# A two-layer gated cross-attention kernel: the first head's operand rows copied by matrix products, the mask's sum moved to GpSimd behind the head loads

## What is computed

```python
qh = (q @ Wq.T + bq); kh = (k @ Wk.T + bk); vh = (v @ Wv.T + bv)   # k = v = ctx, 6404 x 128
attn = softmax(einsum('bhtd,bhsd->bhts', qh, kh) * scale)           # 1024 x 6404 per head
out = einsum('bhts,bhsd->bhtd', attn, vh) @ Wo.T + bo
x = x + tanh(g_xattn) * out                                         # then the experts, gated too
```

## Time and profile before

| | us |
|---|---|
| median of three timed runs (2675.59 to 2676.3) | 2675.84 |
| the profiled execution, its own time | 2680.53 |
| its span, first to last instruction | 2678.5 |
| PE busy | 2498.9 |
| DVE busy | 2157.2 |
| ACT busy | 1935.9 |
| GpSimd busy | 27.6 |

### The profile page before, as it was taken

The page is one execution under the profiler, slowest core; times in us unless marked ns, Lnnn a source line. Parts: engine busy times, 40 slices in busy tenths (PEclk is TensorE's granted clock), DMA queues, the critical chain, the costliest instruction groups (busy, mean ns, idle before and its releaser), DMA issues.

```text
span 2678.5 us, 50842 instructions
## 1 busy us (share of the span) xinstructions
PE 2498.9 (93%) x21050; PEld 959.8 (36%) x21052; DVE 2157.2 (81%) x2215; ACT 1935.9 (72%) x3545; POOL 27.6 (1%) x27
## 2 busy tenths in 40 slices
PE   3379999999999999999796899999999999999989
PEld 1243333333333333334342333333333333333343
DVE  5469999999999999953436899999999999999144
ACT  2058888888888888885331388888888888888932
POOL 4000000000000000000000000000000000000000
PEclk9559999999999999999796799999999999999989
DMA  7120000000000000003100000000000000000000
GB/s 250 69 82 21 29 29 29 29 29 29 28 28 28 29 29 29 22 25 117 54 1 22 4 30 28 28 28 28 28 28 30 29 29 29 28 28 14 1 0 8
DMA packets 36417, 94.36 MB, mean 35 GB/s; under 512 B 4020, under 2 KB 14808, under 8 KB 35928
## 3 DMA queue, kind: packets, MB, share of 16 engines
q1 hardware_dynamic: 34744, 90.69, 9.3%
q10 hardware_dynamic: 1440, 0.40, 0.1%
HBM read 75.08 MB, written 15.74 MB: 34 GB/s over the span
## 4 chain that ended last, share of the span: by engine, by line
PE 63%; DVE 32%; SPq 2%; DMA 1%; issue 1%; ACT 1%; DVEq 0%; ACTq 0%
DVE m_part L657 29%; PE ps L978 22%; PE ps L930 19%; PE ps L949 9%; PE ps L1079 4%; PE ps L1087 3%; SPq L299 1%; PE ps L890 1%; PE ps L920 1%; DMA probs<-in_mask_t 1%; PE ps L882 1%; DVE probs L613 1%; SPq L308 1%; PE ps L992 1%; PE ps L1099 1%
## 5 line engine op out<-in xcount | busy, mean ns | idle before, releaser
L657 DVE TENSOR_REDUCE m_part<-ps 128x2 f32<-128x1024 f32 (+1 forms) x1664 | 1933.1, 1184 | 168.2 <-PE ps L949 164.0
L495 ACT ACTIVATE probs<-ps 128x512 f32<-128x512 f32 (+1 forms) x3264 | 1760.0, 595 | 313.8 <-PE ps L930 197.8
L978 PE MATMUL ps<-probs,v_all 128*9 128x256 f32 x13056 | 1010.8, 382 | 1.6 <-ACT o_raw L475 0.5
L930 PE MATMUL ps<-q_ring,k_ring 35*128 35x512 f32 x3264 | 872.1, 497 | 0.6 <-ACT q_ring L484 0.4
L949 PE MATMUL ps<-k_ring,q_ring 33*128 33x512 f32 (+1 forms) x3328 | 732.2, 419 | 63.2 <-DVE m_part L657 34.6
L930 PEld LDWEIGHTS ps<-q_ring,k_ring 35*128 35x128 f32 x3264 | 348.5, 183 | 709.1 <-ACT probs L495 612.3
L949 PEld LDWEIGHTS ps<-k_ring,q_ring 33*128 33x128 f32 x3328 | 350.0, 194 | 150.7 <-DVE m_part L657 107.1
L978 PEld LDWEIGHTS ps<-probs,v_all 128*9 128x9 f32 x13056 | 195.3, 89 | 549.2 <-ACT probs L495 465.3
L794 DVE TENSOR_TENSOR probs<-probs,ps 128x512 f32<-128x512 f32 x64 | 39.7, 682 | 77.6 <-ACT probs L528 70.1
L528 ACT ACTIVATE probs<-ps,b_col 128x512 f32<-128x512 f32 x64 | 44.0, 687 | 72.3 <-PE ps L1079 72.2
L678 DVE RECIPROCAL r_den<-ps 128x8 f32<-128x8 f32 x32 | 6.6, 207 | 107.0 <-PE ps L957 106.7
(11 more groups left out here) (127 smaller groups left out, 590.3 us busy)
## 6 DMA issues: line engine op xcount, KB each, us to landing
k_ring<-k_parts SPq DMA_DIRECT2D x384, 96.0 KB
k_ring<-k_parts SPq DMA_DIRECT2D x128, 112.2 KB
probs<-in_mask_t SPq DMA_DIRECT2D x10, 640.0 KB, 4.5
k_parts<-probs SPq DMA_DIRECT2D x12, 512.0 KB, 3.1
k_parts<-big SPq DMA_DIRECT2D x12, 512.0 KB, 3.1
q_ring<-q_parts SPq DMA_DIRECT2D x120, 32.0 KB
big<-in_w SPq DMA_DIRECT2D x1, 2048.0 KB, 10.5
q_parts<-probs SPq DMA_DIRECT2D x4, 512.0 KB, 3.5
```

What stands on the lines that cost most here:

```text
L495: A(probs[0:k, n % PSLOTS, HALF * half:HALF * half + HALF], ps[0:k, e_bank(unit), :], ACT.Exp, scale=SCALE).then_inc(sem(f"exp_done{l}"), 1)
L657: V.tensor_reduce(m_part[:, h % 2, :, p, c], mx(n % 2)[:, :, 0:chunk_w[c]], AX.X, ALU.max).then_inc(sem(f"mx_done{l}"), 1)
L930: pe.matmul(bank, k_ring[row:row + ROWS_EXP, koff:koff + P], q_ring[row:row + ROWS_EXP, qoff:qoff + HALF], start=not masked, stop=True).th ...
L978: mm = pe.matmul(ps[32 * g:32 * g + VW, 7, 0:QGW], v_all[:, t, h, :], probs[:, n % PSLOTS, QGW * g:QGW * g + QGW], start=(t == 0), stop=(t ...
```

## The change

1. Head 0's rows of layer 0 no longer pass through HBM. PE multiplies the staged parts by 0/1 matrices (`r_k`, `r_q`, made by GpSimd in `selections`) that put each channel on all its rows (`repeat`), into bank 6, and ACT copies the bank to the ring (`copy_over`), adding the ones row as a bias. The key chunks are made inside the loop of the first units, three chunks ahead. The staging buffers lie in the part of `k_ring` that belongs to head 1.
2. The low part of layer 0's keys is made by GpSimd (`low_keys`) from a second ACT copy with the bias (`k_sum`) instead of by DVE from PSUM.
3. Each attention weight has its own wait (`weight_in`) in place of one for all eight loads; the bias rows of the two layers share one buffer, layer 1's being loaded behind its first head's loads.
4. SP issues the other small loads and the first experts' weights (`setup`) after head 0 and 1's loads, not before.
5. GpSimd clears and sets ring rows only once the normalised x is there, and its other constants come behind the third chunk's low part, with a single semaphore.
6. The mask's pieces are loaded one behind each head's key loads (heads 2 to 12); GpSimd adds them as 32-bit integers and folds the sum to 160 words, DVE totals those.
7. `m_pad` becomes fp32r and the four transposes of the row step become plain fp32r products with an fp32r identity. The PE warming products read `zeros` in place of `probs`.

The diff, cut to its core:

```diff
             def load_first0():
 
-                sp.wait_ge(sem("ring_set"), RING_SET)
-                first_queries(0)
-                store_k(0)
-                keys_stored(0)
-                for g in range(len(K_GROUPS)):
-                    load_keys(0, 0, g)
-                sp.wait_ge(sem("q_stored0"), 16 * 2)
-                load_queries(0, 1)
-                for g in range(len(K_GROUPS)):
+                store_q(0)
+                for g, (c0, c1) in enumerate(K_GROUPS):
+                    store_k(0, c0, c1)
+                    if g == 0:
+                        sp.wait_ge(sem("ring_set"), RING_SET)
+                        sp.wait_ge(sem("q_stored0"), 16 * 2)
+                        load_queries(0, 1)
+                        sp.wait_ge(sem("copied_over"), REPEAT_AT["q"] + 1)
+                        keys_stored(0, c1)
+                        load_keys(0, 1, g)
+                keys_stored(0)
+                sp.wait_ge(sem("copied_over"), NCH + 1)
+                for g in range(1, len(K_GROUPS)):
                     load_keys(0, 1, g)
                 load_queries(0, 2)
...
                         load_keys(l, h, g)
+                    if l == 0 and h - KRING <= NFULL // MCH:
+                        check_mask(h - KRING)
...
+            load_context()
+            load_first0()
             setup()
-            load_first0()
-            check_mask()
             load_heads(0)
...
             constants()
+            for c in range(NCH):
+                low_keys(c)
+                if c == 2:
+                    more_constants()
+                if c == UPPER:
+                    pool.wait_ge(sem("copied_over"), REPEAT_AT["q"] + 1)
+                    pool.wait_ge(sem("q_stored0"), 16 * 2)
+                    set_ones(0, HALF * UPPER, 0)
+            pool.wait_ge(sem("copied_over"), NCH + 1)
+            for n in range(KST):
+                pool.wait_ge(sem(f"k_stored0_{n}"), 16 * len(range(n, NCH, KST)))
+            set_ones(HALF * UPPER, TK, 2)
+            put_mask_together()
...
+            def project_k(c):
+
+                w = chunk_w[c]
+                act.wait_ge(sem("k_proj0"), c + 1)
+                if c >= KST:
+                    act.wait_ge(sem(f"k_stored0_{c % KST}"), 16 * (c // KST))
+                    act.wait_ge(sem("repeated"), REPEAT_AT[c - KST] + 1)
+                A(k_st[0][:, c % KST, 0, 0:w], ps[:, 4 + c % 2, 0:w], ACT.Identity, bias=b_col[:, 0, 1:2]).then_inc(sem("k_evac0"), 1)
+                if c >= 2:
+                    act.wait_ge(sem("k_split0"), c - 1)
+                A(k_sum[:, c % 2, 0:w], ps[:, 4 + c % 2, 0:w], ACT.Identity, bias=b_col[:, 0, 1:2]).then_inc(sem("k_evac0"), 1)
+
+            def copy_over(what):
+
+                act.wait_ge(sem("repeated"), REPEAT_AT[what] + 1)
...
+                    A(k_ring[:, HALF * what:HALF * what + chunk_w[what]], ps[:, 6, 0:chunk_w[what]], ACT.Identity,
+                      bias=one_rows[:, 0:1]).then_inc(sem("copied_over"), 1)
...
-            project_q(0)
-            project_k()
-            for c in range(NCH):
-                set_v(c)
-                if c < NFULL // MCH + 1:
-                    sum_mask(c)
-            act.wait_ge(sem("mask_summed"), NFULL // MCH + 1)
             exp_all(0)
...
             def maxima(l):
-                dve.wait_ge(sem("rank"), E + 4)
+                dve.wait_ge(sem("constants"), 1)
...
+            def repeat(what):
+
+                n = REPEAT_AT[what]
+                pe.wait_ge(sem("selected"), 4 * PARTS)
+                if n:
+                    pe.wait_ge(sem("copied_over"), n)
+                if what == "q":
+                    pe.wait_ge(sem("q_split0"), 2)
+                    for i in range(2 * PARTS):
+                        mm = pe.matmul(ps[:, 6, :], r_q[:, i, :], q_st[0][0:HD, i // PARTS, i % PARTS, :],
+                                       start=(i == 0), stop=(i == 2 * PARTS - 1))
+                else:
+                    pe.wait_ge(sem("k_split0"), what + 1)
...
                     for p in range(NPAIR):
-                        mm = pe.transpose(bank[:, P * p:P * p + P], m_pad[:, p, :], ident_f[:, :])
+                        mm = pe.matmul(bank[:, P * p:P * p + P], m_pad[:, p, :], ident_r[:, :], start=True, stop=True)
...
             def attention(l, masked):
                 for i, unit in enumerate(FIRST_UNITS):
+                    if l == 0 and i % 4 == 0 and i // 4 + 3 < NCH:
+                        keys(0, i // 4 + 3, 4)
+                    if l == 0 and i % 4 == 1 and i // 4 + 2 < NCH:
+                        repeat(i // 4 + 2)
                     m_unit(l, unit, masked)
...
-                    if l == 0 and i % 4 == 3 and i // 4 < NCH:
-                        values(0, i // 4, 4, 4)
+                    if l == 0 and i % 4 == 2 and i // 4 < NCH:
+                        values(0, i // 4, 7, 1)
...
+            turn_queries(0)
+            keys(0, 0, 4)
             queries(0)
-            for c in range(NCH):
-                keys(0, c)
+            keys(0, 1, 4)
+            repeat(0)
+            repeat("q")
+            keys(0, 2, 4)
+            repeat(1)
             attention(0, False)
```

More of the change, by code:

```diff
@@ L78 @@
 K_GROUPS = [(0, 3), (3, 6), (6, 9), (9, KCH)]
+UPPER = 6
+REPEATS = [0, "q"] + list(range(1, KCH))
+REPEAT_AT = {u: n for n, u in enumerate(REPEATS)}
+RING_SET = KRING + 2
+MASK_LEFT = 160
 def max_units(h):
@@ L322, in first_queries @@
                             row = HB * half + (b * PARTS + part) * HD
-                            sp.dma_start(q_ring[row:row + HD, 0:HALF].bitcast(F32), q_st[0:HD, half, part, :].bitcast(F32)
+                            sp.dma_start(q_ring[row:row + HD, 0:HALF].bitcast(F32), q_st[l][0:HD, half, part, :].bitcast(F32)
                                          ).then_inc(query_in(l, 0)[0], 16)
@@ new lines, in put_mask_together @@
+            def put_mask_together():
+                words = mask_sum.bitcast(I32)
+                link(nc.gpsimd.memset(mask_sum, 0.0))
+                for c in range(NFULL // MCH + 1):
+                    pool.wait_ge(sem(f"mask_in{c % 2}"), 16 * (c // 2 + 1))
+                    rows, n = (P, MCH * TQ // 4) if c < NFULL // MCH else (TAIL, TQ // 4)
+                    new = sum_stage[c % 2].bitcast(I32)[0:rows, 0:n]
+                    if c:
+                        pool.wait_ge(sem("mask_met"), c)
+                    nc.gpsimd.tensor_tensor(words[0:rows, 0:n], words[0:rows, 0:n], new, ALU.add).then_inc(sem("mask_met"), 1)
+                pool.wait_ge(sem("mask_met"), NFULL // MCH + 1)
+                n = MCH * TQ // 8
+                while n > MASK_LEFT:
+                    link(nc.gpsimd.tensor_tensor(words[:, 0:n], words[:, 0:n], words[:, n:2 * n], ALU.add))
+                    n //= 2
+                nc.gpsimd.tensor_tensor(words[:, 0:n], words[:, 0:n], words[:, n:2 * n], ALU.add).then_inc(sem("mask_folded"), 1)
@@ L872, in _, with keys @@
         def _(pe):
-            def keys(l, c):
+            def keys(l, c, bank):
                 w = chunk_w[c]
+                if c == 0:
+                    pe.wait_ge(*weight_in(l, "k"))
                 if l == 0:
```

258 lines of the change are left out of this document (163 added, 95 removed).

## The result

The changed kernel takes 2612.97 us (median of four runs, 2605.52 to 2616.61) against 2675.72 for the kernel before beside it: a ratio of 0.9764, 95% interval 0.9742 to 0.9787. (The ratios compare all the repeated runs of both kernels, so they can differ by some tenths of a per cent from the quotient of the medians.) Its profiled execution took 2612.98 with a span of 2611.2, which is 67.3 less than the span of before.

The account below looks back on a forecast made before the run. PE paces most of the span, so the gain must come from the first 190 us: 46 (start) + 33.6 (mask) + (72.9 - 64.7) (units) = 88, less 2 for rows, 86; 2680.5 becomes 2594.5, less 4.7, 2590; range 2576 to 2618.

Parts of the forecast that it names:

- rival (a): Head 0's units: PE's slow clock stays throughout, maxima end at 112, 18 us worse, total 2608; chance 0.17.
- The start: Up to the first reduction: normalised x at 10.3, first reduction at 29 (27 to 33) against 75.11, 46 us earlier.
- The mask: Head 0's units: the 33.6 us halt goes whole; GpSimd's additions, at most 3.3 us each, cost nothing.
- rival (c): GpSimd's mask additions meet DVE's SBUF operations in ten heads: 33 us, total 2623; chance 0.05.
- The row products: Row step, 32 times in the full loop: fp32r products replacing transposes cost between 0 and 16 us; 2 taken.
- rival (b): Row step: the products cost the plain f32 price, 14 us more than taken, total 2604; chance 0.09.
- The pace of the units: Head 0's 52 units: clock rises after one 6.8 us group, then nine at 4.8; 64.7 us in all.
- the 88: End of head 0's maxima: at 94 against 181.62, 88 us earlier, from start, mask halt and units.
- the 4.7 us: Whole kernel: the runs' median stands 4.7 us below the profiled execution, so 2594.5 becomes 2590.
- The low end of the range: Whole kernel: start at 27, all groups at 4.7, no row cost; 98 us gained, 2578, rounded to 2576.
- (d): Head 0's units: the copies' ring through PE, ACT and GpSimd paces the groups, 70 us more, 2660; chance 0.03.
- (e): Loop: warming with zeros fails to lift PE's clock; two heads at 1.2 GHz give 2722, slower than before; chance 0.02.

Follow-up runs that it names:

- before_no_mask_sum: The kernel before without mask loads and sums, the total that picks layer 1's path set by hand: 2642.26 us, ratio 0.9813.
- after_no_mask: The changed kernel without the mask's loads and GpSimd's additions, layer 1's path picked by a constant: 2608.64 us, ratio 0.9722.
- after_again: The changed kernel unaltered, executed once more as a reference: 2612.14 us, ratio 0.9783.
- fill3: The changed kernel with one 512-column bf16 product of zeros ahead of each key chunk, copying product and value chunk, three per group of four units: 2594.83 us, ratio 0.9679.
- constants_first: The changed kernel with GpSimd's other constants made behind the first key chunk's low part instead of the third's: 2606.14 us, ratio 0.9736.
- all_warm: The changed kernel with zero products in unit groups, early constants, warmed last heads, and one warming product behind late layer 0 units and layer 1's first-head units: 2608.43 us.

## Why the prediction was right, and where it was wrong

The forecast was 2590 in a range of 2576 to 2618; 2613 is inside it, 23 above. The direction held, and so did the mechanism of the start and of the mask. The mechanism of the units' pace did not: 2613 is inside because the range was drawn to reach rival (a), whose 2608 is nearer than the forecast.

- **The start: right.** Normalised x 10.49 (10.3 foretold), first reduction 29.77 (29), with the constants last. GpSimd's subtraction took 1.27 us, not 1.0, the constants 26.62 to 29.74, 3.1 and not 3.5. The estimate of 1.1 from the Trainium skill (GPSIMD Engine Reference, section 3.1) was nearer than mine, and still low. A weight did come late: PE's L1049 waited until 13.51 for Wq. I had costed the separate waits at nothing, and it stayed in the range.
- **The mask: right.** Of the halt of 33.59, 32.3 come back where nothing else changes (before_no_mask_sum), and the additions are hidden (after_no_mask): rival (c) didn't happen.
- **The row products: better than taken.** 0 in place of 2: the bound of the 260-wide row was the true one, and rival (b) fell. Its 16 us also came from a misread row: the 1.41 us counts from a weight load at 1237.08 that stands ahead of the products. PE's timeline of the kernel before there:

```profile
1237.51 1.05 PE L890 MATMUL ps<-w_att,ctx_t 128*128 128x128 f32 x8
```

The next product began at 1238.49, so the eight take 0.98 us, 0.39 more than the four transposes and not 0.82.
- **The pace of the units: wrong.** The step that failed is "I expect it to rise after the first group and stay for the nine with key chunks". The clock came up for about 3 us in three of the groups and fell back (in after_again for three groups in a row, in none of these traces for all nine). The price of a group at the full clock was right: 4.8 foretold, 4.83 and 4.87 in after_again. What is more, the pieces at the slow clock were undersized: chunk 2.0 for 1.7, copies 1.14 for 1.0, pairs 0.72 or 0.57 for 0.5, which makes 7.75 and not the 6.8 of rival (a). The last two groups took 5.98, as foretold. From first reduction to end the units took 115.71 - 29.77 = 85.9 us and not 64.7: 21.2 more. With the start's 0.8 that is the 88 that became 65.9.
- The reason given for the step was that the group would be full. It was: PE 77.21 of 80 us busy. The flaw was to let that decide. The row that spoke against it, a clock of 0.50 with PE at 76%, came from the stage next in kind, as the prediction said of rival (a); the full loop is quite another mix of products. Rival (a) had 0.17; it is what happened for the most part, its end of 112 (115.71 measured, 110.45 in after_again) included.
- **The other terms.** From 86 to 67.3 there are 22.1 for the above, 2 back for the row products, 2.15 for head 1, 5.1 back between the layers, 1.6 at the end: 22.1 - 2 + 2.15 - 5.1 + 1.6 = 18.8. Nobody foretold the 5.1, and whether the change has earned it is not shown: that stage took 324.9 to 337.6 us in the traces of the changed kernel and its variants, and 329.2 to 337.2 in those of the kernel before. It is luck that it helped. And the 4.7 us that I took off because before's profiled execution lay above its median did not recur: the changed kernel's two agree. 18.8 + 4.7 is the 23. The low end of the range does not add up either: start at 27, groups at 4.7 and no row cost give 48.1 + 33.6 + 13.8 = 95.5, not 98.
- Rivals (d) and (e) didn't show. The ring of copies was fast enough with DVE pacing at 5.08 us (fill3), and the loop from 140 us on has a clock of 1.00 with zeros as the warming data.

**Open.** Why the clock rises in some groups and not in others, and why three fillers hold it up (a wait of 0.24 us for DVE does not by itself bring it down, as after_again shows); the size of what constants_first gives by itself; what lets it fall in the last head in some executions only.

## What to carry to other kernels

When two pieces of a profile differ in clock, price the new stage at both, and let only a row of the same mix decide: "PE is full" is not such a row. Where PE paces a stage at the lower clock, a few products of zeros between its pieces can be worth more than they cost (three per group of four units gave 14 to 17 us here), but try them stage by stage: in layer 1 a unit became 0.14 us longer by them. And taking away an interference that is plain in the trace (22 us of memsets beside the norm) may pay nothing while what caused it only moves to another place on the path.

## What the runs showed of the hardware

- The granted clock can sit near 0.5 with PE busy for 19.77 of 20 us, and even for 30.00 of 30 (all_warm, layer 1), and stand at 1.00 with 20.00 of 20 (fill3): the busy share of the trace does not tell them apart.
- The two instructions of an fp32 product of 512 columns take 2.07 us at a granted clock of 0.50 and 1.12 at 1.00 (after_again at 70.54 and 65.67).
- An fp32r product of 128 columns costs what an fp32 transpose costs (278 and 273 ns), its weights 192 ns against 140.
- An int32 addition of 1280 words takes GpSimd 2.93 us, and DVE's reductions from PSUM beside it keep their 1.23.
